# Routing inside the first attention batch, and scatters spread over other batches: attention plus a mixture of experts on one Trainium2 core

## The reference

```python
xn = layernorm(x)
# attention: 16 heads of width 8, causal, q and k scaled to length 1
sim = einsum('bhid,bhjd->bhij', l2norm(q), l2norm(k)) * 8.0      # q, k, v = xn @ Wq, Wk, Wv
att = (softmax(where(causal, -max, sim)) @ v) @ Wo
# experts: 8 of them, each row goes to its best two
top_v, top_i = top_k(softmax(xn @ Wr.T), 2)                       # weights: top_v / sum(top_v)
y_e = gelu(xn @ W1[e].T + b1[e]) @ W2[e].T + b2[e]                # 128 -> 512 -> 128
out = x + att + sum over e of y_e * w_e
```

## Time and profile before

| | |
|---|---|
| median of 3 runs | 798.06 us (797.99 to 802.88) |
| the profiled execution | 802.14 us, its span 800.4 us |
| mean granted clock of TensorE | 0.949 of 2.4 GHz |
| busy: TensorE | 716.7 us, 90% of the span |
| busy: ScalarE, VectorE, GpSimd | 495.4, 491.1 and 431.9 us |
| chain that ended last | TensorE 42% of the span, ScalarE 3% |
| longest groups: exponentials (L674) | 311.0 us, 1034 ns each |
| times v (L795) | 180.5 us |
| expert matmuls (L934, L946) | 138.8 and 138.5 us |
| scatters (L546) | 128, 985 ns each |

### The profile page before, as it was taken

How to read it: one execution, slowest core, us unless ns; L and a number is a source line. 1 busy time by engine, 2 the same in 40 slices (tenths; PEclk the granted TensorE clock), 3 DMA queues, 4 the chain that set the end, 5 groups by cost and what they waited for, 6 DMA issues and landing times. The chain is left out here.

```text
span 800.4 us, 19383 instructions
## 1 busy us (share of the span) xinstructions
PE 716.7 (90%) x6151; PEld 447.5 (56%) x6151; DVE 491.1 (61%) x1318; ACT 495.4 (62%) x833; POOL 431.9 (54%) x558
## 2 busy tenths in 40 slices
PE   2777659999999998999979999999989999999986
PEld 2555512333333334999969999999953333333333
DVE  7799795566556754444424444667645766677743
ACT  2566537788887875444424444444457888887873
POOL 4444417666666667576620016476525666666672
PEclk9888859999999998999989999999989999999998
DMA  7665548443354236644422224344414544444331
GB/s 207 211 211 177 171 113 192 82 85 76 92 97 102 66 83 142 204 143 126 141 66 66 72 79 112 99 117 112 111 39 80 70 96 101 100 113 116 65 93 34
DMA packets 170117, 89.20 MB, mean 111 GB/s; under 512 B 77104, under 2 KB 159824, under 8 KB 170064
## 3 DMA queue, kind: packets, MB, share of 16 engines
q1 hardware_dynamic: 161872, 71.74, 36.4%
q0 software_dynamic: 8192, 16.79, 7.3%
HBM read 39.47 MB, written 32.24 MB: 90 GB/s over the span
## 5 line engine op out<-in xcount | busy, mean ns | idle before, releaser
L674 ACT ACTIVATE prob<-psum 128x1024 f32<-128x1024 f32 x320 | 311.0, 1034 | 89.1 <-PE psum L770 83.8
L686 ACT ACTIVATE prob<-psum,prob 128x256 f32<-128x256 f32 x284 | 117.6, 471 | 157.6 <-PE psum L934 156.7
L795 PE MATMUL psum<-prob,v 128*18 128x384 f32 (+2 forms) x2560 | 180.5, 390 | 2.0 <-POOL prob L564 1.0
L557 POOL TENSOR_SCALAR_AFFINE_SELECT prob<-prob 128x512 f32<-128x512 f32 x128 | 88.1, 688 | 134.2 <-ACT prob L674 133.9
L546 POOL DMA_INDIRECT slot_x<-rows,idx x128 | 126.1, 985 | 48.8 <-issue 29.5
L544 POOL DMA_INDIRECT rows<-slot_y,idx x128 | 123.2, 963 | 53.5 <-issue 25.7
L770 PE MATMUL psum<-qks 32*128 32x512 f16 (+3 forms) x1024 | 126.3, 307 | 23.8 <-ACT prob L674 17.7
L946 PEld LDWEIGHTS psum<-prob 128*128 128x128 f32 x1136 | 138.4, 192 | 3.7
L934 PE MATMUL psum<-xs,prob 128*128 128x256 f32 x568 | 138.8, 388 | 0.0
L946 PE MATMUL psum<-prob 128*128 128x128 f32 x1136 | 138.5, 275 | 0.0
L770 PEld LDWEIGHTS psum<-qks 32*128 32x128 f16 x1024 | 33.9, 92 | 162.7 <-ACT prob L674 105.5
(11 more groups left out here) (146 smaller groups left out, 744.5 us busy)
## 6 DMA issues: line engine op xcount, KB each, us to landing
xs<-slot_x SPq DMA_DIRECT2D x71, 128.0 KB
slot_y<-xs SPq DMA_DIRECT2D x71, 128.0 KB
xs<-in_L_attn_x SPq DMA_DIRECT2D x16, 256.0 KB, 3.3
prob<-in_L_ffn_W SPq DMA_DIRECT2D x16, 256.0 KB, 3.1
xn_rows<-xns SPq DMA_DIRECT2D x16, 256.0 KB, 3.5
xn_cols<-xts SPq DMA_DIRECT2D x16, 256.0 KB, 3.5
xt<-xn_cols SPq DMA_DIRECT2D x16, 256.0 KB, 3.5
rows<-xn_rows SPq DMA_DIRECT2D x16, 256.0 KB, 3.2
```

The lines of the kernel that those rows point to most:

```text
L557: pool.affine_select(out=p, in_=p, compare_op=ALU.is_ge, fill=0.0, base=0, pattern=[[0, 2], [0, 2], [1, P]], channel_multiplier=-1).then_i ...
L674: act.activation(prob[:, q % 2, KEPT[u], :], score[(q + u) % 2], ACT.Exp, scale=SCALE / UP ** 2).then_inc(exp_done, 1)
L686: act.activation(hs[:, s, c, :], psum[:, 2 * s + c // 2, (c % 2) * FT:(c % 2 + 1) * FT], ACT.Gelu, bias=ws[:, s, B1C + c:B1C + c + 1]).the ...
L795: mm = pe.matmul(ps_o[32 * g:32 * g + VW, first:first + cols], lhs, prob[:, w % 2, KEPT[u], c:c + cols], start=(i == 0 and not odd), stop= ...
```

## The change

- VectorE prepares all four tiles of batch 0 ahead of the last selection, and SyncE turns them ahead of everything else. Counting, ranking and what follows move into `body(0)` of TensorE and VectorE: `count_tokens` and `place_tokens` into group 0, `segments` (the chain to `last_i`) into group 1, `places` into group 2, `find_slots` into group 3. `pick` and the plan of the tiles move into batch 1.
- Counts have a PSUM bank of their own (`ps_count`).
- GpSimd moves no rows in batch 0. The 24 moves of batches 0 to 2 stand in batches 1 and 2, one and two to a slot in turn. Batch 7 moves its own rows in slots 0 to 3, two to a slot, and in slots 4 to 7 the first four of batch 8; `between` begins with the other four.
- `load_rows(2)` stands ahead of the fourth turning of batch 2 and not behind all four.

```diff
@@ SyncE, start of the attention
-            for s in range(2):
-                for par in range(2):
-                    sp.wait_ge(cols_out[par][s], 16 * (NB // 4))
-                sp.wait_ge(rows_out[s], 16 * (NB // 2))
...
-            sp.wait_ge(norms_ready, NB)
-            load_rows(0, 0)
-            load_rows(1, 1)
-            load_xt(1)
...
             for t in range(TB):
                 turn_qk(0, t, 0)
 
+            for s in range(2):
+                for par in range(2):
+                    sp.wait_ge(cols_out[par][s], 16 * (NB // 4))
+                sp.wait_ge(rows_out[s], 16 * (NB // 2))
+            load_xt(1)
+            sp.wait_ge(norms_ready, NB)
+            load_rows(0, 0)
+            load_rows(1, 1)
             sp.wait_ge(zeroed, 16)
             sp.wait_ge(lasts_ready, 1)
@@ SyncE, body
                     for t in range(TB):
+                        if known(b, 1) and t == TB - 1:
+                            load_rows(b + 1, 1 - par)
                         turn_qk(b + 1, t, 1 - par)
...
                 if not second:
-                    if not known(b, 0):
+                    if not (known(b, 0) or known(b, 1)):
                         load_rows(b + 1, 1 - par)
@@ GpSimd, body and between
-                        if known(b, 0) and slot == 3:
+                        if known(b, 1) and slot == 0:
                             pool.wait_ge(routed, 1)
                             pool.wait_ge(padded, 16 * E)
-                        order = [0], [1], [2], [3], [4], [5], [6], [7]
+                        order = [(b, par, slot)]
                         if known(b, 0):
-                            order = [], [], [], [0, 1], [2, 3], [4, 5], [6], [7]
+                            order = []
+                        if known(b, 1) or known(b, 2):
+                            first = 3 * MOVES // 2 * (b - 1) + 3 * slot // 2
+                            order = [(k // MOVES, k // MOVES % 2, k % MOVES)
+                                     for k in range(first, first + 3 * (slot + 1) // 2 - 3 * slot // 2)]
+                        if known(b, HALF - 1):
+                            order = [(b, par, 2 * slot), (b, par, 2 * slot + 1)] if slot < MOVES // 2 else \
+                                [(HALF, 0, slot - MOVES // 2)]
...
-                with pool.Fori(HALF // 2, NB // 2) as i:
+                for j in range(2):
+                    for o in range(MOVES // 2 if j == 0 else 0, MOVES):
+                        move(HALF + j, j, o, False)
+                with pool.Fori(HALF // 2 + 1, NB // 2) as i:
@@ TensorE, body(0) and body(1)
+                    if known(b, 0) and w == 3:
+                        pe.wait_ge(ranks_read, 2)
...
-                    if known(b, 0) and w == 1:
+                    if known(b, 1) and w == 2:
                         pe.wait_ge(pick_ready, 1)
...
                     scores(b, par, w, 2)
+                    if known(b, 0) and w == 0:
+                        count_tokens()
...
                         if w == 0:
                             project(b + 1, 0)
+                            if known(b, 0):
+                                place_tokens()
@@ VectorE
-            prepare(0, 0, 0)
-            prepare(0, 0, 1)
+            for t in range(TB):
+                prepare(0, 0, t)
             for c in range(TOPK):
                 select(T // ST - 1, c)
...
                     elif w == 1:
...
+                        if known(b, 0):
+                            segments()
                         if not last:
                             prepare(b + 1, 1 - par, 1)
...
                     elif w == 2:
                         if not last:
+                            if known(b, 0):
+                                places()
                             prepare(b + 1, 1 - par, 2)
...
+                    if known(b, 0) and w == 3:
+                        find_slots()
+                    if known(b, 1) and w == 0:
+                        pick_tiles()
+                    if known(b, 1) and w == 1:
                         write_plan()
```

More of the change, by code:

```diff
@@ L1125, in _ @@
             dve.wait_ge(counted, 1)
-            dve.tensor_copy(totals.rearrange("p c n -> p (c n)"), ps_o).then_inc(totals_read, 1)
-            for t in range(2, TB):
-                prepare(0, 0, t)
-            dve.wait_ge(counted, 2)
+            dve.tensor_copy(totals.rearrange("p c n -> p (c n)"), ps_count).then_inc(totals_read, 1)
+            dve.memset(ps_o, 0.0).then_inc(cleared, 1)
             def stepped(ins):
@@ L1185, in _ @@
-            for c in range(TOPK):
-                dve.tensor_tensor(mine, hot[:, c], place, ALU.mult).then_inc(r_step, 1)
-                dve.wait_ge(r_step, next_step())
-                with nc.allow_low_precision(reason="one number that isn't zero, and whole"):
-                    dve.tensor_reduce(slots[:, :, c], mine, AX.X, ALU.add).then_inc(r_step, 1)
-                dve.wait_ge(r_step, next_step())
-            dve.memset(ps_o, 0.0).then_inc(r_step, 1)
-            dve.wait_ge(r_step, next_step())
@@ new lines, in find_slots @@
+            def find_slots():
+                for c in range(TOPK):
+                    dve.tensor_tensor(mine, hot[:, c], place, ALU.mult).then_inc(r_step, 1)
+                    dve.wait_ge(r_step, next_step())
+                    with nc.allow_low_precision(reason="one number that isn't zero, and whole"):
+                        dve.tensor_reduce(slots[:, :, c], mine, AX.X, ALU.add).then_inc(r_step, 1)
+                    dve.wait_ge(r_step, next_step())
+                dve.sem_inc(routed, 1)
```

172 lines of the change are left out of this document (92 added, 80 removed).

## The result

| | before | changed |
|---|---|---|
| median, first comparison | 800.32 us (4 runs, 797.99 to 802.88) | 817.60 us (4 runs, 816.92 to 817.97) |
| ratio | | 1.023, 95% interval 1.0196 to 1.0264 |
| median, second comparison, another chip | 798.22 us (11 runs, 796.83 to 803.33) | 818.50 us (4 runs, 818.09 to 818.93) |
| ratio | | 1.0253, 95% interval 1.0236 to 1.0271 |
| profiled execution, span, clock | 802.14, 800.4, 0.949 | 816.92, 815.2, 0.946 |

The kernel is slower, by 2.3 to 2.5%. Against the profiled execution of before the difference is 14.8 us, where the sum said 14.1. Against the median it is 17 to 20 us, where the prediction said 14: 812 was forecast and 817.6 to 818.5 measured, inside the range of 804 to 818 but for the second chip's half microsecond.

What follows compares the result with a forecast made beforehand. TensorE, busy 90% of the span, gains only where it idles or runs at the lower clock. Terms 4.9 + 0.4 + 0.5 + 6.0 + 2.3 = 14.1 us on the 798.06 us median gave 812, range 804 to 818.

Steps and rivals of the forecast that it cites:

- the same sum on the median gives 812: Last step: the 14.1 us give 816.2 on the profiled execution of 802.14, and 812 on the median of 798.06.
- Batch 2: Start of batch 2: its fourth turning waits behind batch 0's last scatter on GpSimd; +0.5 us, between 0 and 2.
- batch 1's start: Batch 1 waits for turnings behind `last_i`, fills and the `acc` load in SyncE's queue: 140.4 against 135.5, +4.9 us.
- batch 7: GpSimd waits for batch 8's row load, issued behind four turnings; TensorE waits for a mask: +6.0 us, lower-clock restart +2.3.
- The restart of batch 1: After idling, TensorE restarts batch 1 at the lower clock: 2.35 us, of which 1.95 already lost before; +0.4 us.
- The start: Batch 0's first score 5.5 us earlier, at 101.4; `last_i` at 114.7; batch 0's gain absorbed in the wait for batch 1.
- Rival A: The 7.20 us hold of batch 1's first turning doesn't recur: -2.0 in place of +4.9, 805 us; chance 0.08.
- Rival C: Batch 1 isn't held by SyncE's queue and starts at 129.5, 6.0 us early: 801 us, not slower; chance 0.05.
- Batches 1 and 2 on GpSimd: 12 scatters in each batch fill GpSimd, but masks are ready about 2.1 us before use: costed at nothing.
- Rival D: GpSimd falls behind in batches 1 and 2 with 1.35 us scatters; TensorE waits some 7 us: 819 us; chance 0.05.
- Rival B: In batch 7, TensorE doesn't feel the row load of batch 8: 8.3 us less, 804 us; chance 0.07.
- The seam and the late wait: Attention's end to first expert matmul, and the 5.58 us wait for last scattered rows: neither gives time back; 0, at most 0.3.

Runs made afterwards that it cites:

- h1: The kernel before, unchanged, profiled again to get a short execution: 796.54 us profiled, median of ten 797.52 us.
- e3: Changed kernel with the 2 MB load of `acc` issued behind batch 1's turnings and the load of `xt`: 895.06 us, 1.0089 of the kernel before, slow-expert chip.
- i1: As i2, but with batch 7's scatters as they were before the change: 790.93 us against 798.31 for the kernel before (0.9891).
- i2: As f4, plus the eight zero fills interleaved with batch 1's turnings: 791.00 us against 798.31 for the kernel before (0.9905).
- f1: The changed kernel, unchanged, repeated beside the kernel before on the same chip: 818.50 us against 798.22.
- f2: Kernel before with only batch 7's part of the change (its new scatter places): 808.27 us, 1.0135 of the kernel before.
- e2: Changed kernel with batch 8's row load issued ahead of its four turnings: 891.30 us, 1.0024 of the kernel before, slow-expert chip.
- f4: Changed kernel, batch 8's row load ahead of its turnings, `acc` load behind batch 1's, row loads of batches 10 to 15 two expert tiles earlier: 795.19 us (0.9946).
- f3: Changed kernel with batch 7's scatters as they were before: 808.21 us, 1.012 of the kernel before.
- the e and g runs: Runs of the kernel before and of variants on two chips where every kernel needs some 72 to 91 us more among the experts.

## Why the prediction was right or wrong, point by point

**The step that failed is the last one of the sum: "the same sum on the median gives 812".** The 14.1 us were worked out against a long execution and then added to the median of short ones. That is allowed only if both kernels have the 4 us that lie between. They don't: the changed kernel's eight executions all lie within 2.1 us, 816.9 to 818.9. On the profiled execution the sum came out (816.2 against 816.92), with errors that cancel; on the median it had to be 20.

**Two terms were mis-sized most.** Batch 2 stood at +0.5 and cost 3.0, against the long execution and against h1. The experts stood at 0 and took 1.0 and 2.5 us more. Term by term, with batch 1's start of h1 at 133.30 + 0.4 = 133.7 and the middle of a batch at its third group (146.92, 171.26 and 195.61 in h1, 150.15, 174.50 and 198.85 in the long execution):

| term | predicted | changed less long | changed less h1 |
|---|---|---|---|
| batch 1's start | +4.9 | 138.94 - 135.5 = +3.4 | +5.2 |
| from there to the middle of batch 1 | +0.4 | 14.19 - 14.65 = -0.5 | 14.19 - 13.22 = +1.0 |
| to the middle of batch 2 | +0.5 | 27.36 - 24.35 = +3.0 | 27.36 - 24.34 = +3.0 |
| to the middle of batch 3 | 0 | 24.49 - 24.35 = +0.1 | +0.1 |
| batch 7 | +6.0, +2.3 | +8.8 | +8.8 |
| experts | 0 | +1.0 | +2.5 |
| second half | 0 | -1.1 | -0.3 |
| sum | 14.1 | 14.8 | 20.4 |

**The restart of batch 1** was charged in part only. I took a loss of 1.95 us that batch 1 "has already" from the earlier trace rows and charged the 0.4 above it. The typical execution has hardly any. From the six 256-wide score matmuls that end batch 0 to the group in the middle of batch 1 it is 150.15 - 135.02 = 15.13 us in the long execution and 146.92 - 133.30 = 13.62 in h1. Against h1 the changed kernel loses 1.0 there, so this made 0.6 us of the error.

**The start** was right in its mechanism: first score 101.4 predicted, 100.41 measured; `last_i` 114.7 and 114.17. The fourth turning went out at 135.6, 21.4 us behind `last_i` and not 22.5, so batch 1 began at 138.94 and not at 140.4: the term was 1.5 us too large. TensorE was through with batch 0 at 126.4 and not at 128.6, which the wait took up, as said. Rival A (the hold doesn't recur) is out: 7.01 us again, and gone in e3, where nothing stands in front. Rival C (batch 1 not held) is out by the 12.55 us of idleness; even with the load moved 5.6 stay.

**Batch 2** I had at +0.5, between 0 and 2. The mechanism was right: GpSimd's eighth scatter ended at 160.19, SyncE then issued the row load and the fourth turning, and batch 2 began 28.1 us after batch 1 (167.06 - 138.94), where I had 27.1. But TensorE wanted it after 25.8 and not after 26.7, since batch 1 had lost less at its restart. So it waited 2.33 us, above the upper end of what I gave, and restarted at the lower clock, which I had not charged (granted 0.90 and 0.93 in the rows above): 3.0 in all. Every kernel that carries the change's start has this cost, 27.0 to 28.8 us from middle to middle, the fastest ones (i1, i2) too. No run moves this row load alone, so the share of its order is read from the rows and not tested.

**Batches 1 and 2 on GpSimd** cost nothing, as said. Rival D asked for some 7 us of TensorE's waiting for a mask; the waits behind the two batches are 2.33 and, at the start of batch 3, 0.76 us (none in f1), both for turnings. The 22 scatters from 139 to 192 us took 1.03 us on the mean, against 0.97 assumed and 1.35 in D. The Trainium skill's rule that VectorE's two-port copies lock GpSimd out (SBUF — State Buffer, section SBUF: two separate sides), which the prediction set beside D, explains at most these 0.06 us.

**Batch 7** was right: GpSimd stands 6.97 us for the row load, TensorE 5.89 for a mask (6.0 predicted), and 8.8 in all (8.3 predicted). f2 makes it alone, and the order of the load takes the wait away (e2). What it leaves is some 1.3 us of the stretch (f4 and i2 against i1), the cost of the new places of the scatters. Rival B is out.

**The seam and the late wait** gave nothing back, as said: 2.83 us for the copy of `xs`, 5.61 for the last rows. From the end of the attention to the first expert matmul it is 4.2 us, as before. What I missed are 2.5 us among the experts: the first two tiles take 8.63 us (8.70 in f1) against 7.22 in h1, at the lower clock, and 0.7 more lie around the late wait. The held batch 7 by itself does not make it, nor does the change of the start: the first two tiles take 7.44 us in f2 and 7.39 in f3, but 8.23 in the long execution of before, which has neither. What does stays open.

**What was not tried:** the row load of batch 2 behind its turnings again, with all else of the change; and whether the fall-back of the clock in a long execution can be set off on purpose.

## What to carry to other kernels

Before a sum is carried from a profiled execution to a median, ask of which kind that execution was: take a second profile, or charge each restart in full and say which execution it is charged against. And when work moves between batches, go through every queue that feeds it: here both large holds and the late wait lay in SyncE's order of issues (a row load behind four turnings, turnings behind a 2 MB load, row loads two tiles late), and so, by the rows, did the 3 us of batch 2 (a turning behind a row load that waits for GpSimd).

## What the runs showed of the hardware

- An issue of a transposing DMA behind a 2 MB load in the same queue holds the queue: the one right behind it takes 7.01 and 7.20 us, all four 11.55 (changed) or 12.00 (before), against 6.21 without the load in front (e3).
- TensorE's granted clock can fall to 1.2 GHz in one execution and not in another of the same program, with nearly the same work in front of it (8.65 and 9.03 us busy from 130 to 140; granted 0.93 and then 0.90 against 1.00). This one fall costs 1.5 us; with a later start and slower restarts a long execution takes 5.6 us more than h1, more than most terms of the sum.
- Chips differ. On two of them (the e and g runs) the kernel before takes 888 to 891 us, with 360 to 366 us for the experts instead of 274 to 276. Between expert tiles VectorE and ScalarE stand for something that the profile calls remote. What it is stays open. The two stretches of the attention's first half are as long as elsewhere within 2 to 4 us.
